# An attention block on one core: products of zeros at the start, the queries' weights split earlier, first projections and maxima in another order

## What is computed

```python
x_n = _group_norm(x, gn_w, gn_b)
q = _conv1x1(x_n, wq, bq)
k = _conv1x1(x_n, wk, bk)
v = _conv1x1(x_n, wv, bv)
...
attn = jnp.einsum('bhqd,bhkd->bhqk', q, k) * scale
attn = jax.nn.softmax(attn, axis=-1)
out = jnp.einsum('bhqk,bhkd->bhqd', attn, v)
...
return x + _conv1x1(out, wp, bp)
```

## Time and profile before

| | us |
|---|---|
| three executions | 366.38, 367.43, 367.86 (median 367.43) |
| the profiled execution | 366.56 |
| its span, first to last instruction | 364.8 |
| PE busy in it | 348.0 (95%) |
| first projection to first scores | 12.96 to 28.32 |

### The profile page before, as it was taken

One profiled execution on the slowest core, in us unless ns is written; L12 is line 12 of the kernel. 1 busy time (PEld: TensorE's weight loads), 2 busy tenths in 40 slices (PEclk: granted clock), 3 DMA queues, 4 the chain that ended last, 5 costly groups with the idle time before them and its releaser, 6 DMA issues.

```text
span 364.8 us, 11244 instructions
## 1 busy us (share of the span) xinstructions
PE 348.0 (95%) x4577; PEld 208.6 (57%) x4577; DVE 284.0 (78%) x447; ACT 303.1 (83%) x362; POOL 284.2 (78%) x258
## 2 busy tenths in 40 slices
PE   0899999999999999999999999999999999999996
PEld 0544565655656556655666556565656556655564
DVE  5788899878887787778887777777877787787474
ACT  1748879898877999989878999998889888888982
POOL 5066888699788997998778997998879797967722
PEclk9999999999999999999999999999999999999999
DMA  6055141213743341143553241031552441070113
GB/s 212 19 146 144 45 97 38 30 62 103 135 142 74 80 98 43 24 112 116 124 154 66 60 106 64 10 80 43 117 164 53 94 85 65 2 202 3 31 31 118
DMA packets 38587, 30.92 MB, mean 85 GB/s; under 512 B 23676, under 2 KB 31368, under 8 KB 38536
## 3 DMA queue, kind: packets, MB, share of 16 engines
q1 hardware_dynamic: 37792, 29.15, 32.6%
q10 hardware_dynamic: 744, 1.06, 0.8%
HBM read 9.44 MB, written 4.19 MB: 37 GB/s over the span
## 4 chain that ended last, share of the span: by engine, by line
PE 85%; DVE 8%; ACT 2%; issue 2%; DMA 1%; DVEq 1%; ACTq 0%
PE gen L617 19%; PE st L743 14%; PE st L744 14%; PE pv L766 9%; PE pv L769 8%; PE pv L768 7%; PE st L709 5%; PE mx L709 3%; DVE mx L1053 3%; DVE p_lo L1086 2%; ACT st L969 1%; DVE mx L1049 1%; PE st L617 1%; PE mx L824 1%; DMA xin<-in_x_dram 1%
## 5 line engine op out<-in xcount | busy, mean ns | idle before, releaser
L964 ACT ACTIVATE p_hi<-st 128x1024 f16<-128x1024 f32 x127 | 130.7, 1029 | 40.2 <-PE st L744 38.8
L1328 POOL TENSOR_TENSOR p_lo<-p,p_hi 128x1024 f16<-128x1024 f32 x62 | 132.3, 2133 | 10.4 <-ACT p L969 10.4
L766 PEld LDWEIGHTS pv<-v_hi,p_hi 128*128 128x128 f16 x1024 | 93.4, 97 | 26.7 <-issue 15.0
L766 PE MATMUL pv<-v_hi,p_hi 128*128 128x65 f16 x1024 | 106.4, 195 | 0.3 <-DVE o L1094 0.2
L768 PE MATMUL pv<-v_lo,p_hi 128*128 128x64 f16 x1024 | 105.9, 193 | 0.0
L769 PE MATMUL pv<-v_hi,p_lo 128*128 128x65 f16 x1024 | 105.7, 194 | 0.0
L1086 DVE TENSOR_TENSOR p_lo<-st,p_hi 128x512 f16<-128x512 f32 x126 | 80.8, 683 | 30.0 <-ACT st L969 29.7
L743 PE MATMUL st<-q_twice,k_both 128*128 128x512 f16 x256 | 97.0, 379 | 1.6 <-DVE p_lo L1086 1.2
L768 PEld LDWEIGHTS pv<-v_lo,p_hi 128*128 128x128 f16 x1024 | 93.8, 98 | 6.2
L744 PE MATMUL st<-q_max,k_one 65*128 65x512 f16 x256 | 97.3, 380 | 0.0
L769 PEld LDWEIGHTS pv<-v_hi,p_lo 128*128 128x128 f16 x1024 | 93.9, 97 | 0.0
(11 more groups left out here) (200 smaller groups left out, 558.4 us busy)
## 6 DMA issues: line engine op xcount, KB each, us to landing
q_twice<-st_hi_q SPq DMA_DIRECT2D x64, 64.0 KB, 2.1
xres<-in_x_dram SPq DMA_DIRECT2D x4, 1024.0 KB, 5.2
out_dram<-y SPq DMA_DIRECT2D x13, 256.0 KB, 2.3
xin<-in_x_dram SPq DMA_DIRECT2D x6, 512.0 KB, 4.6
k_both<-st_hi_k SPq DMA_DIRECT2D x16, 128.0 KB, 2.3
k_one<-st_hi_k SPq DMA_DIRECT2D x16, 128.0 KB, 2.6
q_max<-st_lo_q SPq DMA_DIRECT2D x32, 64.0 KB, 2.1
k_both<-st_lo_k SPq DMA_DIRECT2D x16, 128.0 KB, 2.3
```

The costliest lines, as they stand in the source:

```text
L766: nc.tensor.matmul(pv_v[:, q, :], hi, vh, start=k == 0 and q == 0, stop=False, skip_group_check=True)
L964: nc.scalar.activation(p_hi[:, G % PR, :, :], scores, ACT.Exp, scale=SM_SCALE / M_SCALE)
L1328: nc.gpsimd.tensor_tensor(p_lo[:, G % PR, :, :], p_full(G), p_hi[:, G % PR, :, :], ALU.subtract)\
```

## The change

Before anything else PE multiplies a tile of zeros by itself 28 times (`EARLY`); the tile is `turn`, which DVE zeroes first, with a semaphore of its own. The queries' weights are transposed between the products for mean and variance; ACT writes their high part ahead of `veps`, DVE their low part right behind the deviations. ACT writes the values' weights ahead of z, and the last weights behind z. The first products take the two channel tiles in turn, with the low part of the queries' weights at once. ACT evicts both high parts first and the full ones after them. The tables of jobs and maxima are replaced by code: `second_keys`, `second_queries` and `first_values` put one maximum (at one place two) after each piece of a projection; maxima (1, 2) and (1, 3) move behind the first scores.

```diff
+            pe.wait_ge(s_turn_zero, 1)
+            for n in range(EARLY):
+                nc.tensor.matmul(first_banks[0][:, 0:2 * P], blank[:, 0:P], blank[:, 0:2 * P], start=True, stop=True)
             pe.wait_ge(s_const, 2)
...
-            for kind in ("mean", "var"):
-                job(kind, 0, 0, 0, stat_banks[kind])
+            job("mean", 0, 0, 0, stat_banks["mean"])
             transpose_weights(0, "q")
+            job("var", 0, 0, 0, stat_banks["var"])
             transpose_weights(1, "k")
...
             first_products()
-            for n, ((kind, i, j), bank) in enumerate(zip(FIRST_JOBS, first_banks)):
...
+            second_keys()
+            second_queries()
+            first_values()
+            first_maximum(1, 0)
+            pe.wait_ge(s_e32["k"], 2)
+            job("k", 1, 0, 0, first_banks[5], between=turn_shift)
+            first_maximum(1, 1)
```

The new functions on PE:

```diff
             def first_products():
...
                 for t in range(CT):
+                    pe.wait_ge(s_z0_hi, t + 1)
+                    for m, kind in enumerate("qk"):
+                        pe.wait_ge(s_whi, m + 1)
+                        product(kind, 0, w_hi, z_hi, t, start=t == 0)
+                        if kind == "q":
+                            pe.wait_ge(s_wlo, 1)
+                            product(kind, 0, w_lo, z_hi, t)
                 for t in range(CT):
+                    pe.wait_ge(s_z0_lo, t + 1)
+                    last = product("q", 0, w_hi, z_lo, t, stop=t == CT - 1)
+                    if t == CT - 1:
+                        last.then_inc(s_gen_full, 1)
+                    product("k", 0, w_hi, z_lo, t)
                 pe.wait_ge(s_wlo, 2)
...
+            def second_keys():
+
+                for t in range(CT):
+                    pe.wait_ge(s_z0_hi, CT + t + 1)
+                    product("k", 1, w_hi, z_hi, t, start=t == 0)
+                    product("k", 1, w_lo, z_hi, t)
+                pe.wait_ge(s_z0_lo, CT + 1)
+                product("k", 1, w_hi, z_lo, 0)
+                first_maximum(0, 0)
+                first_maximum(0, 1)
+                pe.wait_ge(s_z0_lo, CT + 2)
+                product("k", 1, w_hi, z_lo, 1, stop=True).then_inc(s_gen_full, 1)
+
+            def second_queries():
+
+                for t in range(CT):
+                    product("q", 1, w_hi, z_hi, t, start=t == 0)
+                    product("q", 1, w_lo, z_hi, t)
+                    first_maximum(0, 2 + t)
+                product("q", 1, w_hi, z_lo, 0)
+                product("q", 1, w_hi, z_lo, 1, stop=True).then_inc(s_gen_full, 1)
+                first_maximum(0, 4)
+
+            def first_values():
+
+                pe.wait_ge(s_wlo, 3)
+                for c in range(4):
...
+                        first_maximum(0, 5 + c)
```

On ACT and DVE:

```diff
+            split_weights(0)
             job("var", 0, 0, 0, stat_banks["var"])
-            split_weights(0)
             split_weights(1)
+            split_weights(2)
             first_z_high(0)
             first_z_high(1)
-            split_weights(2)
+            split_weights(3)
             act.wait_ge(s_col_sc, 4)
...
+            for kind, bank in zip("qk", first_banks):
+                bank_full()
+                first_high(kind, bank)
+            for kind, bank in zip("qk", first_banks):
+                first_full(kind, bank)
...
             first_about_group_mean()
+            split_weights(0)
             dve.wait_ge(s_col_sc, 4)
...
             first_z(0)
-            first_z_low(0, 0)
-            split_weights(0)
-            first_z_low(0, 1)
+            first_z_low(0, 0, 1)
             split_weights(1)
```

More of the change, by code:

```diff
@@ L619, in part, with job @@
                 return last
-            def job(kind, i, j, b, bank=gen, only=None, midway=(), between=None):
+            def job(kind, i, j, b, bank=gen, only=None, between=None):
                 if kind in "kqv" and (b > 0 or kind == "v"):
@@ L638, in job @@
                                     lambda t: (z_hi[:, b % 2, t, half], z_lo[:, b % 2, t, half]), n)
[L639 to L643 removed]
+                        if n == 0 and between:
+                            between()
                     if kind == "v":
@@ new lines, in second_queries @@
+            def second_queries():
[9 more added lines that the diff above has]
+                for c in range(4):
+                    k = slice(c * P, (c + 1) * P)
+                    for t in range(CT):
+                        last = part(gen[:, c * P:(c + 1) * P], lambda t: (z_hi[:, 0, t, k], z_lo[:, 0, t, k]),
+                                    lambda t: (w_hi["v"][:, t, 0:P], w_lo["v"][:, t, 0:P]), t, first=c == 0)
+                    if c == 3:
+                        last.then_inc(s_gen_full, 1)
+                        held.append(("v", 0, 0, 0))
+                    else:
+                        first_maximum(0, 5 + c)
```

70 lines of the change are left out of this document (27 added, 43 removed).

## The result

The changed kernel takes 364.58 us, the median of nine executions (364.39 to 365.70), beside 367.17 for the kernel before in nine (365.96 to 367.86): a measured ratio of 0.9943, 95% interval 0.9930 to 0.9956 (the two medians alone make 0.9929). It is faster by 0.57%, and the interval lies on the faster side of no change. The profiled execution took 364.64, its span is 362.9, against 364.8 before. Among the experiments, one execution of e11 took 877.34 us; it counts as slow and is left out of e11's times and ratio.

The account below looks back on a forecast made before the run. TensorE is fully busy from 39 us, so only an earlier hand-over from the head could gain. Terms 0 - 0.57 - 1.21 - 0.25 = -2.03 off the median 367.43 gave 365.4 us, range 363.6 to 366.8.

Parts of the forecast that it names:

- the interleave: Second keys' products and maxima alternated in the head: the idle stretch between the two groups of reductions goes, -1.21 us.
- the moved pair: Two maxima put behind the first scores: less idling on VectorE before the second unit's shift, -0.25 us, bounds 0 and 1.29.
- the spacing of the first projections: Sign right after the first projection: 512-column products 0.43 us apart if the forecast holds, 0.21 if the clock stays up.
- first rival: Head: the clock stays up from the zeros to the projections, -2.8 us off the profiled time, 363.8 us; chance 0.25.
- the second unit's shift: Sign at the end of the head: it comes about 2 us before 34.43, otherwise the prediction is wrong.
- Zeros, and the clock: Kernel start: 28 zero products end by 7.2 us within TensorE's idleness, cost nothing, and leave the projections' clock down.
- I take that it is not: Step: the clock is no longer up at the first projections, near 12.9 us, some 5.6 us after the last zero product.
- forecast case: First projections meet the clock down, 0.43 us per product; the sum comes off the median, 365.4 us; chance 0.55.
- Queries' weights between mean and variance: Head, ahead of the projections: earlier transposes and split move veps by between +0.5 and -0.25 us; taken as 0.
- ACT's order: Evictions after the first projections: high keys written 0.57 us earlier, first reduction at 18.0 for 18.59, -0.57 us.
- The low keys' transfer: Rival: the first scores wait for it; held up by 1 to 2 us, the time is 366.4 to 367.4; chance 0.12.
- The zeros at 0.43 each: Rival at the kernel start: zero products end at 13.4 us and hold up the statistics, 371.0 us, slower; chance 0.08.

Follow-up runs that it names:

- e11: The kernel before with 28 products of zeros of 1 column at the start and nothing else; 366.01 us, ratio 0.9996.
- e7: The changed kernel with the order of first projections and maxima of the kernel before put back; 365.29 us, ratio 0.9951.
- e3: The changed kernel with maxima (1, 2) and (1, 3) put back ahead of the first scores; 364.17 us, ratio 0.9928.
- e4: The changed kernel with the values' products moved from between the maxima into slot 0, behind maxima (1, 2) and (1, 3); 364.08 us, ratio 0.9930.
- e5: The changed kernel with the next image's first statistics put behind the reductions of (1, 0) and (1, 1); 365.70 us, ratio 0.9959.
- e8: The changed kernel with maxima (1, 2) and (1, 3) ahead of the first scores and 38 zero products instead of 28; 364.88 us, ratio 0.9945.
- e10: The changed kernel with maxima (1, 2) and (1, 3) ahead of the first scores and the values' products behind them in slot 0; 365.38 us.
- e12: The changed kernel with maxima (1, 2), (1, 3) ahead of the first scores and (1, 1) ahead of turning the shift; 363.43 us, ratio 0.9911.
- e6: The kernel before with only the queries' weights transposed between mean and variance and split earlier; 366.82 us, ratio 0.9996.
- e1: The changed kernel without its products of zeros; 365.62 us, ratio 0.9963.
- e2: The kernel before with the 28 products of zeros and nothing else of the change; 365.43 us, ratio 0.9964.

## Why the prediction was right, and where it was not

Forecast 365.4, range 363.6 to 366.8, most of the chance on faster; measured 364.58. The sum was -2.03, the spans differ by 1.95. The sum came out near, but its terms did not, and that it came out near is luck: the interleave and the moved pair brought 1.21 less than forecast, the first reduction came 0.50 sooner than forecast, and 0.57 came from a place that was not in the sum.

By its own signs the prediction holds in part. The reductions do not idle between the fourth and the fifth beyond 0.18, and the first scores start 2.85 sooner. But the spacing of the first projections was the first rival's (0.21, not 0.43), the case that had been given a chance of 0.25. And the second unit's shift stands 1.32 before 34.43, not about 2, which had been named as a sign of being wrong.

**Zeros, and the clock.** That they fit into PE's idle time was right: 5.42 for 28, done 1.3 ahead of the mean. The step "I take that it is not", that the clock is down again at the first projections, failed for the changed kernel: all twelve products stand at 0.22. Both grounds for it were too thin. The clock did fall, at 9.2; but it rose again by 12.6, and PE did nothing but the end of the variance and transposes in between. The Trainium skill, "TensorE: Matmul & The Clock Gate", section "Part 4: PE-mode transpose", has it that a transpose does not count as activity for the full clock; the windows of the changed kernel speak against it, the trace of e7 does not. In e3, e4, e5, e8 and e10 the clock did not even fall. PE's timeline of e5, whose zeros end at 5.98, has the last four transposes at the high rate (0.63, where the low rate has 1.06), and PEclk is 1.00 from 7 to 16:

```profile
10.28 0.63 PE L812 MATMUL pv<-ident,w_in_p 128*128 128x128 f32 x4
12.20 0.39 PE L838 MATMUL st<-z_hi,w_hi_q 128*128 128x512 f16 x1 [1.30 <-ACT z_hi L1046]
```

So a stretch with little but transposes, 6.2 us here, need not bring the clock down, as the end of the kernel, where PE does nothing at all, had made me expect. The prediction let the rule on transposes and the earlier trace rows support each other, though the earlier trace rows only showed that 4.4 us of transposes had not raised the clock *yet*. e7's profiled execution shows that the forecast case exists; of the nine profiled kernels with zeros of 256 columns it is the only one with the first projections at 0.43. Why executions differ in this stays open. Where the fall came made 0.24 in A: the changed kernel's variance took 0.55 in it (A 9.53), in e12 it took 0.38 and was over when the clock fell (A 9.29).

**Queries' weights between mean and variance.** Taken as 0 between -0.25 and +0.5. veps is at 9.68, and 9.69 before, with a mean that starts 0.23 later: the lower end, because the clock was up for the transposes (0.64 for four). The upper end was set too high: by the earlier trace rows four transposes at the low rate take 1.1 and not the 1.25 of the sum (8.35 to 9.6), and without zeros e6 and e1 have veps only 0.15 later after the mean than before. DVE's low split did go into its wait for POOL; that wait is 0.28 now, for 1.44.

**ACT's order, -0.57.** The size was right: at like clock A is 0.53 and 0.43 shorter (e1). But the first reduction came 1.07 sooner, as the clock was not like before's. The reasoning of the rival "clock stays up" had it: then DVE sets the pace, and the reduction starts where the low split of the values ends, at 17.25 by the prediction, 17.52 with 0.23 of later input. In the forecast case, by e7, A was 0.27 shorter, not 0.57, with a clock that rose some three products later than before's.

**Interleave, -1.21.** This is the term that was mis-sized: 0.40, by B and by e7. The stretch of 1.21 did go. But "a maximum has 1.3 us per bank to be replaced, and needs 0.4" looked at the banks alone, and not at PE's own row: six products of the values stand between two maxima, and PE issues a maximum each 0.78 us (20.06, 20.84). The last four reductions take 0.42 longer than before, and with two waits of 0.18 ahead of them, at maxima that stand behind products of the second queries, that is 0.78 of the lost 0.81. e4 shows the first part by taking the values' products out (B 0.47 shorter); the two waits of 0.18 stay there.

**Two maxima behind the first scores, -0.25.** Wrong in sign: +0.15 in C. "The bottom is 0 since each maximum still waits for a free bank" overlooked that DVE can then wait for the moved pair (0.62 ahead of (1, 2)), with every later step of DVE behind it: a bottom of 0 was no bottom. e3 undoes it and gains 0.41.

**What was not in the sum.** -0.57 in the tail. I had looked for what the zeros cost, not at what 56 more instructions of PE move. The Trainium skill, "Runtime: NRT & Kernel Launch", section "Instruction fetch mechanics", says that code is refilled in blocks of 16 KiB by a DMA queue of the sequencer's own, and that crossing a block is mostly hidden. The sizes agree with the 37 packets here (14 more, on a second instruction queue, are of 8 KB). Hidden it is not where a short transfer on which PE waits, or the last store, shares the moment: 3.3 us for 2.0 in e8.

**The rivals.** The clock up was the case of the profile, yet 363.8 was too low by 0.8: its first reduction was right, and the two terms above were wrong in it too. The low keys' transfer ended no wait in the changed kernel's profile: the first scores at 25.47 (forecast 24.7) stand right behind the maximum at 25.13, so PE's own row sets them. The zeros at 0.43 each did not happen.

## What to carry to other kernels

Where one engine makes items and another consumes them through two buffers, count the maker's row between two items, with all that stands between them, and not only the buffers' round. Earlier first work is worth only what the last wait of the hand-over lets through: e3 starts its first scores later than the changed kernel (26.35 for 25.47) and is ahead of it from slot 1 on, so put the feeding of the engine that paces (here DVE, C) first. And compare variants piece by piece from a common event: the input's arrival, the clock and the place of code packets each moved single profiles by 0.5 us and more, as much as the edits did.

## What the runs showed of the hardware

- In the changed kernel the granted clock came back to 1.00 by 12.6 after the end of the variance and twelve transposes at 0.50; in e7 it was still at 0.50 at 16.1, after the same transposes and nine projections, and in e5 it stayed at 1.00 through all sixteen transposes. It also fell inside the head, where PE had products between its waits: at 19.6 to 22.8 in e2, after projections and the first maxima, and at 28.4 to 31.6 in e5, after scores and maxima. Executions of one kernel differ in it. PEclk reads 1.00 in e1 from 12.60 to 13.40 too, where products are 0.40 to 0.43 apart, as in the earlier trace rows: ahead of the first recorded change the spacing tells the level.
- A packet of code of 16 KB, one of 37 in a span, delays what is moved beside it: 1 KB took 3.3 us instead of 2.0 (e8; 2.64 to 3.97 in the 89 slow ones of 434 such transfers, each of which meets a packet), a store of 256 KB 2.8 instead of 2.0 (before). Which transfer it meets depends on the number of instructions ahead of it, so in e8's profiled execution ten products that cost nothing in the head cost 1.00 us some 120 us later.
- Six values products and a maximum take PE 0.78 where the products' own spacings (six of 0.056) and a maximum's 0.22 make 0.56: some 0.1 goes at each change between products of 64 and of 128 rows (a maximum and its neighbours); the scores' products of 65 and 128 rows follow one another every 0.22, without it (25.47, 25.69, 25.91 in the changed kernel).
